# A sparse two-expert network on one core: standing weights for the chunks of a known expert, and slot numbers made by the vector engine

## The reference

```
logits = xf @ router_w.T                       # 576 x 8
top_logits, top_idx = top_k(logits, 2)
top_w = softmax(top_logits)
for e in range(8):
    w_e = sum(top_w * (top_idx == e))
    h = silu(xf @ Wg[e].T) * (xf @ Wu[e].T)    # 192 -> 768
    out = out + h @ Wd[e].T * w_e[:, None]     # 768 -> 192
return h_in + out
```

## Time and profile before

| | |
|---|---|
| median of 3 runs | 223.16 us (222.1 to 223.44) |
| the profiled execution's own time | 223.32 us |
| its span | 221.4 us |
| PE busy | 187.0 us (84%), 1534 instructions |
| DVE busy | 147.7 us (67%), 487 instructions |
| ACT busy | 135.9 us (61%), 314 instructions |
| POOL busy | 131.9 us (60%), 187 instructions |

### The profile page before, as it was taken

How to read it: one execution, slowest core, us unless ns; L and a number is a source line. 1 busy time by engine, 2 the same in 40 slices (tenths; PEclk the granted TensorE clock), 3 DMA queues, 4 the chain that set the end, 5 groups by cost and what they waited for, 6 DMA issues and landing times.

```text
span 221.4 us, 4824 instructions
## 1 busy us (share of the span) xinstructions
PE 187.0 (84%) x1534; PEld 148.6 (67%) x1548; DVE 147.7 (67%) x487; ACT 135.9 (61%) x314; POOL 131.9 (60%) x187
## 2 busy tenths in 40 slices
PE   0699979989989949387489999899999999999950
PEld 0699969989978837365337677566677767767630
DVE  1669677989289787998758978576755544444420
ACT  0753686767889788958477777546544444444430
POOL 8205785997688985669988977556222222222222
PEclk9999999999999976675558999999999999999995
DMA  5999998939972283575695768663411122322111
GB/s 155 360 399 364 223 428 297 396 86 390 301 212 46 63 239 101 152 205 135 182 275 166 238 154 182 186 151 62 114 19 19 12 28 42 45 42 45 18 18 18
DMA packets 20416, 36.32 MB, mean 164 GB/s; under 512 B 3817, under 2 KB 10281, under 8 KB 20009
## 3 DMA queue, kind: packets, MB, share of 16 engines
q1 hardware_dynamic: 17449, 33.26, 48.1%
q0 software_dynamic: 2944, 2.76, 8.7%
HBM read 31.65 MB, written 4.36 MB: 163 GB/s over the span
## 4 chain that ended last, share of the span: by engine, by line
PE 45%; ACT 16%; DVE 14%; POOL 9%; issue 9%; DMA 5%; POOLq 1%; ACTq 0%; DVEq 0%
PE ps L1228 6%; PE ps L1413 5%; PE ps L1416 4%; PE ps L1423 4%; PE ps L1411 4%; PE ps L1415 4%; ACT experts L704 4%; POOL h L540 4%; DMA stage<-w_exp 4%; ACT L760 3%; PE ps L1380 3%; PE ps L1412 3%; PE ps L1437 3%; PE ps L1439 3%; PE ps L1438 3%
## 5 line engine op out<-in xcount | busy, mean ns | idle before, releaser
L1228 PE MATMUL ps<-experts 128*117 128x193 f32 (+1 forms) x320 | 58.8, 344 | 7.7 <-DVE experts L963 6.2
L1228 PEld LDWEIGHTS ps<-experts 128*117 128x117 f32 (+1 forms) x320 | 55.7, 191 | 8.9 <-DMA experts<-x_t 7.7
L413 POOL TENSOR_TENSOR experts<-stage,experts 128x528 bf16<-128x528 f32 x38 | 44.5, 1199 | 9.8 <-ACT experts L704 9.8
L1170 DVE TENSOR_TENSOR shared<-shared,ps 128x256 f32<-128x256 f32 x48 | 20.2, 420 | 36.2 <-ACT shared L851 33.7
L704 ACT CAST experts<-stage 128x528 f16<-128x528 f32 x64 | 38.8, 632 | 0.6 <-DMA stage<-w_exp 0.6
L851 ACT ACTIVATE shared<-ps 128x256 f32<-128x256 f32 x48 | 18.6, 387 | 31.3 <-PE ps L1416 30.4
L650 POOL DMA_INDIRECT out<-shared x8 | 12.4, 1545 | 29.8 <-ACT shared L876 27.0
L688 ACT ACTIVATE experts<-experts 128x468 f32<-128x468 f32 x39 | 22.4, 589 | 5.6 <-POOL experts L540 3.3
L650 POOL DMA_INDIRECT out<-shared,slot_row x8 | 13.0, 1625 | 21.1 <-ACT shared L876 20.5
L1437 PE MATMUL ps<-experts,shared 128*128 128x192 f16 (+1 forms) x96 | 23.7, 246 | 1.9 <-DVE shared L1175 1.9
L540 POOL TENSOR_TENSOR experts<-experts 128x468 f32<-128x468 f32 x14 | 16.5, 1180 | 14.4 <-DVE experts L963 9.1
(11 more groups left out here) (240 smaller groups left out, 359.9 us busy)
## 6 DMA issues: line engine op xcount, KB each, us to landing
stage<-w_exp SPq DMA_DIRECT2D x64, 264.0 KB, 3.2
experts<-x_t SPq DMA_DIRECT2D x3, 1888.0 KB, 8.7
experts<-w_proj SPq DMA_DIRECT2D x8, 384.0 KB, 6.5
experts<-x_t SPq DMA_DIRECT2D x8, 236.0 KB, 7.0
experts<-x_t SPq DMA_DIRECT2D x2, 944.0 KB, 5.8
slot_x<-experts SPq DMA_DIRECT2D x1, 1032.0 KB, 8.9
shared<-slot_x SPq DMA_DIRECT2D x8, 129.0 KB, 2.2
out<-h SPq DMA_DIRECT2D x1, 351.0 KB
```

The costliest lines, as they stand in the source:

```text
L413: ops.tensor_tensor(lo_w[:, to + EW:to + EW + PW], stage[:, n % STAGES, :], hi_w[:, to:to + PW], ALU.subtract).then_inc(split_pool if on_p ...
L1228: last = mm(dst, xbuf[:, t % 2, k, 0:m], gw[:, k, :], start=k == 0, stop=k == KT - 1)
```

## The change

It has four parts.

1. For chunks 0 to 7 `gate_up` swaps its operands: blocks of 128 weights stand and the 128 tokens move. There are 20 matmuls of 128 columns in place of 5 of 512, and the result has hidden units on the partitions. `gate` writes it into the bank where the transposes went, and for those 24 steps `turn_hidden` is gone.
2. The slot numbers and facts are computed by VectorE, right after its second pick and before its first pieces of weights and its first `gate`, partly in a spare bank of PSUM. The expert word alone stays on GpSimd.
3. GpSimd's order becomes: eight scatters, `add_out(0)`, two scatters, `add_out(1)`, the word, the other `add_out`s.
4. GpSimd takes 40 pieces of weights in place of 38. VectorE begins with piece 40, takes two before its first step as before, and two a step only while `n` is below 2. ScalarE's order of pieces stays.

```diff
-    POOL_PIECES = 38
+    POOL_PIECES = 40
...
+    OWN = E * STEPS
+    def hid_at(n):
+        return pcol(4 + n % 2, 0, BLK)
...
-            (GpSimd's list of small instructions, lines 574 to 631)
+            def expert_word():
+                pool.wait_ge(ends_ready, 1)
+                (11 small instructions, from cmp to wordi).then_inc(word_ready, 1)
             pool.wait_ge(blank_out, 48)
-            pool.wait_ge(xs_ready, len(GROUPS))
+            pool.wait_ge(slots_ready, 1)
+            pool.wait_ge(xs_ready, 1)
+            scatter_rows(0, 4)
+            pool.wait_ge(xs_ready, 2)
+            scatter_rows(4, 8)
             pool.wait_ge(out_base, 32)
             add_out(0)
-            scatter_rows(0, 2)
+            pool.wait_ge(xs_ready, len(GROUPS))
+            scatter_rows(8, 10)
             add_out(1)
-            scatter_rows(2, 5)
...
+            expert_word()
+            for c in range(2, CHUNKS):
                 add_out(c)
...
             def hidden_high(n):
-                sc.wait_ge(hidT_done, n + 1)
+                if n < OWN:
+                    sc.wait_ge(hid_ready, n + 1)
+                    if n >= 2:
+                        sc.wait_ge(down_step, n - 1)
+                else:
+                    sc.wait_ge(hidT_done, n - OWN + 1)
...
-            link(v.tensor_scalar(wsel[0:TOK, 2, :], gexp[0:TOK, :], 1.0, None, ALU.add))
-            v.reciprocal(wsel[0:TOK, 0, :], wsel[0:TOK, 2, :]).then_inc(share_ready, 1)
+            (33 small VectorE instructions, 12 of them linked, that is, waited for before the next:
+             share, meta, fulls, mores, ends, base, slot, posm, posf, posi, the last with slots_ready)
...
             def gate(n):
                 dve.wait_ge(act_ready, n + 1)
-                if n >= 2:
-                    dve.wait_ge(hidT_done, n - 1)
-                v.tensor_tensor(hid[:, n % 2, :], ...)
+                if n >= OWN + 2:
+                    dve.wait_ge(hidT_done, n - OWN - 1)
+                elif 2 <= n < OWN:
+                    dve.wait_ge(hh_ready, n - 1)
+                    dve.wait_ge(hidT_ready, n - 1)
+                dst = hid_at(n) if n < OWN else hid[:, n % 2, :]
...
-                for _ in range(2 if n < 4 else 1):
+                for _ in range(2 if n < 2 else 1):
...
             def gate_up(n, off):
+                if c < E:
+                    for j in range(2 * HT):
+                        dst = pcol(n % 3, j * P, CHUNK)
+                        mm(dst, part_w(0, off, k1 + j * P, P), x1h[:, c % 2, 0, :], start=True, stop=False)
+                        mm(dst, part_w(1, off, k1 + j * P, P), x1h[:, c % 2, 0, :], start=False, stop=False)
+                        mm(dst, part_w(0, off, k1 + j * P, P), x1l[:, c % 2, :], start=False, stop=False)
+                        mm(dst, part_w(0, off, k2 + j * P, P), x1h[:, c % 2, 1, :], start=False, stop=False)
+                        last = mm(dst, part_w(1, off, k2 + j * P, P), x1h[:, c % 2, 1, :], start=False, stop=True)
...
+                if r == 0 and c == 1:
+                    pe.wait_ge(slots_ready, 1)
...
-                if n >= 1:
+                if n > OWN:
                     turn_hidden(n - 1)
```

More of the change, by code:

```diff
@@ L575, in _ @@
             rests(35, POOL_PIECES)
[L576 to L606, removed]
@@ L613, in _ @@
[L613 to L623, removed]
-            link(g.tensor_tensor(posm[0:TOK, :, :, 0:2], posm[0:TOK, :, :, 0:2], posm[0:TOK, :, :, 2:4], ALU.add))
-            g.tensor_copy(wordi[:, :], word[:, :]).then_inc(word_ready, 1)
-            link(g.tensor_tensor(posf[0:TOK], posm[0:TOK, :, :, 0], posm[0:TOK, :, :, 1], ALU.add))
@@ L627, in _ @@
-            link(g.tensor_copy(posi[0:TOK, :, :], posf[0:TOK, :, :]))
-            for k in range(2):
-                last = g.tensor_copy(xs[0:TOK, :, k, ROW - 1:ROW].rearrange("p t o -> p (t o)"), wsel[0:TOK, k, :])
-            link(last)
             def scatter_rows(n0, n1):
@@ new lines, in over, with along @@
+            def over(w):
+                return spread(w.rearrange("p (o e) -> p o e", o=1), 1, TILES)
+            def along(w):
+                return spread(w.rearrange("p (t o) -> p t o", o=1), 2, E)
+            counts = pcol(6, te, E)
+            near, far = ranks[0:TOK], by_expert(beside(te))
+            total, share, second = beside(TILES), beside(TILES), beside(TILES)
+            both, slot = by_expert(beside(te)), by_expert(beside(te))
+            fulls, mores, ends = beside(E, P), beside(E, P), beside(E, P)
@@ new lines, in _ @@
+            v.reciprocal(share, total)
+            link(v.tensor_scalar(fulls, fulls, MAGIC, None, ALU.add))
+            v.tensor_tensor(second, share, gexp[0:TOK, :], ALU.mult)
+            v.tensor_scalar(base[:, :], fulls, MAGIC, 0.0, ALU.subtract, ALU.max)
+            v.tensor_scalar(mores, fulls, MAGIC, 0.0, ALU.subtract, ALU.max)
+            link(v.tensor_scalar(more_s, fulls, MAGIC, 0.0, ALU.subtract, ALU.max))
+            v.tensor_tensor(both, hot[0:TOK, 0], along(share), ALU.mult)
@@ new lines, in _ @@
+            v.tensor_tensor(wboth[0:TOK, 1], hot[0:TOK, 1], along(second), ALU.mult)
+            v.tensor_copy(xs[0:TOK, :, 0, ROW - 1:ROW].rearrange("p t o -> p (t o)"), share)
+            v.tensor_copy(xs[0:TOK, :, 1, ROW - 1:ROW].rearrange("p t o -> p (t o)"), second)
+            v.tensor_tensor(ends, mores, cum[:, 0, HALF - 1:HALF - 1 + E], ALU.add)
+            link(v.tensor_tensor(ends_s, mores, cum[:, 0, HALF - 1:HALF - 1 + E], ALU.add))
+            v.tensor_tensor(both, both, wboth[0:TOK, 1], ALU.add)
@@ new lines, in _ @@
+            link(v.tensor_tensor(fulls, ends, base[:, :], ALU.subtract))
+            v.tensor_scalar(meta[0:TOK, :, :, 2], wboth[0:TOK, 0], 4096.0, None, ALU.mult).then_inc(meta_ready, 1)
+            link(v.scalar_tensor_tensor(base[:, :], fulls, float(CHUNK), away[:, :], ALU.mult, ALU.add))
+            link(v.tensor_tensor(far, far, over(base[0:TOK, :]), ALU.mult))
+            link(v.tensor_tensor(slot, far, posm[0:TOK, 1], ALU.add))
+            for k in range(2):
+                last = v.tensor_tensor(posm[0:TOK, k], hot[0:TOK, k], slot, ALU.mult)
```

75 lines of the change are left out of this document (47 added, 28 removed).

## The result

In the measurement that the forecast is held against the changed kernel took **224.31 us** (median of 20 runs, 222.06 to 228.32), the kernel before 223.42 (20 runs, 222.04 to 226.36): a ratio of 1.0061, 95% interval [1.0035, 1.0086]. The ratios in this document leave out executions in a slower state of the core, so they are not the quotients of the medians; that quotient is 1.004 here. The forecast was 220.3, 218.2 to 223.1. In five later sets of runs, on four chips, the same two kernels came out the other way round, 218.5 to 219.0 against 220.6 to 221.0. On which chip the first measurement was made is not on record. Most of this document is about that difference.

The account below looks back on a forecast made before the run. The bound changes by stage: TensorE in undisturbed steps, with stalls from late silu releases, and VectorE in the changed start. From 223.32 us, -3.2 (steps) -1.7 (stalls) +1.9 (start) = -3.0 gave 220.3, range 218.2 to 223.1.

Parts of the forecast that it names:

- Standing weights: TensorE's known steps: gate_up at 1.14 us, a step at 1.64 instead of 1.80, saving 3.2 us over 19 steps.
- G(5): Start of the first matmul of gate_up(5) on TensorE; forecast near 126.6 us, before 124.69.
- The rival in which the loads show through: In the 24 gate_ups, weight loads do not hide behind matmuls: a step costs 0.66 us more, 236 in all; chance 0.08.
- The start: First steps: slot numbers on VectorE and a piece waiting for ScalarE's cast delay gate_up(5); costs 1.9 us, bounds 0.6 to 2.6.
- Order of GpSimd and the word: GpSimd's reordered scatters and word: neither rows nor word was late for TensorE, so the gain is 0.
- Stalls: Late silu releases in steps 11, 14 and 17, linked to GpSimd's scatters, would go: 1.7 us gained, uncertain from 0 to 1.7.
- a rival in which the late releases stay: The delay in steps 11, 14 and 17 belongs to something other than scatters; 1.7 us stay, 222.0; chance 0.20.
- the clock falls in the new gap: TensorE, thinly busy from 118.0 to 123.9 us, runs at a lower clock, costing 2.5 us, 222.8; chance 0.14.

Follow-up runs that it names:

- b_again: The kernel before, unchanged, run and traced again on another chip; 220.07 us, ratio 0.9987 to the kernel before.
- r_after: The changed kernel, unchanged, run and traced a second time; 218.81 us, ratio 0.9895 to the kernel before.
- r_after2: The changed kernel, unchanged, traced a third time, on another chip; 218.67 us, ratio 0.9886 to the kernel before.
- b_third: The kernel before, unchanged, run and traced once more on a fourth chip; 220.34 us, ratio 0.9987 to the kernel before.
- old_order: The changed kernel with scatters at their old places between the add_outs and the word behind add_out(1); 223.46 us, ratio 1.0125 to the kernel before.
- late_scatter: The changed kernel with its first eight scatters held back until down(3) is done; 224.22 us, ratio 1.0181 to the kernel before.

## Why the prediction was wrong

**Standing weights: right.** Forecast 1.14 for a `gate_up` and 1.64 for a step; measured 1.12 and 1.61. Over the 19 steps from G(5) to G(24): 39.7 in b_again, 36.2 in r_after, -3.5 where -3.2 was forecast. The rival in which the loads show through is out: at full clock a pair takes 56 ns in every trace of the new `gate_up`. The Trainium skill, TensorE: Matmul & The Clock Gate, section Back-to-back issue gap, gives 81 ns for such a pair; the trace does not agree.

**The start: right where the clock comes back late.** Forecast +1.9, by a piece of VectorE's waiting for ScalarE's cast ahead of `gate(1)`; the wait is there, 1.7 to 1.9 us in r_after and r_after2, and the start takes 14.2 to 14.3 in three traces, against 12.3 to 12.4 in the three of the kernel before. In the two traces of the changed kernel with an early clock (back at full speed 2.6 and 2.9 us behind G(0)) it takes 13.2; the kernel before has no trace with one. The wait is only part of the cost: undoing part 4 gives back 1.1. G(5) was forecast at 126.6, which is 14.2 behind the G(0) of before.

**Order of GpSimd and the word: nothing, as forecast.** The kernel before with part 1 alone has the old order and the faster chunks and waits for no rows. What has little slack is GpSimd's list in the changed kernel: with the word ahead of eight scatters it costs 4 us, with the first scatters held back 5.4.

**Stalls: this step failed.** "The 1.7 us of stalls I count as gone, because each of the three steps with the delay has two or three scatters of GpSimd around its `gate_up`." In b_again and b_third the scatters are there and the stalls are not. They belong to the first measurement, not to the kernel. The forecast called this term its weakest, but it read a coincidence in one trace as a cause. Counted at nothing, the sum is -3.2 + 1.9 = -1.3, and the five later sets of runs show -1.6 to -2.3 us (medians 218.5 to 219.0 against 220.6 to 221.0), with -1.4 to -1.7 between G(0) and G(24) in three traces and -2.5 to -2.7 in the two with an early clock. So where both kernels run undisturbed, the two large terms make the result, and the third was never there. That 218.5 to 219.0 lies inside the forecast range is partly luck: it was counted from a base of 223.3, which was itself 2.5 us long.

**What the forecast had no case for** is that such stalls come in the changed kernel too, and longer. It had a rival in which the late releases stay (1.7 us), none in which they grow. The median of 20 runs was 0.9 us above the kernel before. The two traces of that measurement differ by 0.8, made up of -1.6 (the change, undisturbed), +3.1 (5.6 us lost in the changed kernel, 2.5 in the one before), and -0.7 in G(0). Both medians of 20 runs, 223.42 and 224.31, lie by these traces, and even the shortest of the 40, 222.04 and 222.06, are above every later median of these two kernels. So it was no accident of single executions, but something that held through that measurement; most of the 40 will have lost as much. That is an inference, as of the whole measurement only the two have a trace. One number on record supports it for the changed kernel: the mean granted clock of an execution is 0.910 in the paused trace and 0.920 in r_after. It was 0.912 or less in 16 of the first 20 executions and in none of the 32 later ones (0.913 to 0.928). The rival "the clock falls in the new gap" named the right engine and nearly the right size, but the wrong place: in r_after the gap from 118 to 123 is there and the granted clock stays at 1.00; it fell behind the pauses.

**What stays open** is what holds the engines up. Shown: in the changed kernel's first trace `silu(3)` is released 5.5 us late and `silu(8)` 1.1 us late, and TensorE pauses between two matmuls of one group in the same stretch; in the first trace of the kernel before a release comes 0.7 us late three times; and none of 15 later traces on four chips, five of them of the changed kernel as it is, has either between G(0) and the end of the steps. So neither kernel makes it by itself. That pauses and late releases are one thing is likely, as they stand in one stretch and ScalarE's began first, but it is not shown. Full DMA engines alone don't make it. Not tested: whether the chip of the first measurement, or what ran beside it, does. A few later executions were long as well (222.87 and 222.58 for the changed kernel, 223.56 and 223.78 for the one before), without a trace that would tell why. Not told apart: whether the changed kernel, with its 320 more matmuls or with scatters beside the weights, suffers more from it than the kernel before. The ratio of 1.0061 says that it did in those runs; no later trace brought it back.

**The better kernel.** Part 1 alone, 216.25, 217.0 and 217.33 us on three chips (ratios 0.9824, 0.9839 and 0.9896), is faster than the kernel before in all three. Its medians are 1.2 to 2.6 us below the changed kernel's of the same sets, and G(0) to G(24) is 48.0 to 48.4 against 49.4 to 50.6; the intervals of the ratios overlap, and in the third set its ratio is no better (0.9896 against 0.9873). It was not among the runs of the first measurement.

## What to carry to other kernels

Before a stall is counted as a gain, take a second trace of the same kernel: a release that comes 0.7 us late behind work that nothing held may be gone in the next set of runs, and then it goes into the range, on both sides, and not into the sum. When the list of one engine is moved against that of another, look for the first item that now waits for its partner, here one piece of weights, which with the rest of part 4 gave back about 1 of 3.5 us. Where two traces of a start are compared, look first when the clock came back in each: that was worth 1 us here, as much as the part under test. When an engine stands still, look at the others in the same stretch: here ScalarE had stopped before TensorE did. Cost the parts apart: one of four was the gain.

## What the runs showed of the hardware

- Standing weights cost next to nothing extra at 128 columns: 20 pairs of load and matmul go every 56 ns, against 216 ns for 512 columns in the old form; 20 x 128 and 5 x 512 columns take 1.12 and 1.08 us (changed kernel and r_after; kernel before).
- A wait of 2.4 us in full work (old_order) brought the granted clock from 1.00 to 0.50 for 3.4 us, and cost 1.6 us more than the wait. In r_after TensorE was busy 0.52 of the 2 us from 118 to 120, and the clock stayed at 1.00.
- In one trace ScalarE was released 5.5 us late, and TensorE paused 0.5 to 1.2 us between two matmuls with no releaser, four times in 3.5 us; GpSimd went on. In 15 later traces that never came.
- The time from the first matmul of the steps until the clock was back differed between traces of one kernel, 2.6 to 5.9 us, and was worth 1 us.
- An accumulating scatter of 128 rows that waits for the one before goes every 4.3 us: 1.55 on GpSimd and 2.75 to its landing (late_scatter).
